# Gated delta rule on one core: four-wide inverse products, outputs taken chunk by chunk, two projection banks

## Chip, cores and metric

One core of one Trainium2 chip runs the whole program. The metric is device time in microseconds, the median of several runs. The kernel is written in a low-level language: every engine has its own list of instructions, and semaphores are written out by hand.

## What is computed

The reference is one transformer layer with post-layernorm on x of 2 x 2048 x 256, in float32. The part that the change touches is the attention, a gated delta rule over 16 heads of width 64:

```python
q, k, v = x @ Wq.T, x @ Wk.T, x @ Wv.T
q, k, v = causal_dwconv4(q), causal_dwconv4(k), causal_dwconv4(v)
g, beta = log_sigmoid(x @ Wg.T), sigmoid(x @ Wb.T)
k = k / norm(k);  q = q * 64 ** -0.5
def step(S, inp):                       # one token, S is 64 x 64 a head
    Sk = einsum('bhkv,bhk->bhv', S, k_t)
    delta = outer(v_t, k_t) - outer(Sk, k_t)
    S = exp(g_t) * S + b_t * delta
    return S, einsum('bhkv,bhk->bhv', S, q_t)
x = layernorm(x + o @ Wo.T)
x = layernorm(x + ffn(x))               # 64 experts, top 6, capacity 128, and a shared expert
```

## The kernel before, in words

The program runs five phases one after the other: gates, the delta rule, a mix phase (output projection, layernorm, routing), the experts, and the combination. The change is in the delta phase alone.

**Macros and slots.** The delta rule is computed in chunks of 64 tokens. A macro m is one pair of heads, both batches, and a span of 256 tokens: 4 chunks x 2 heads x 2 batches = 16 blocks of 64 x 64. There are 64 macros. The program is a software pipeline of 71 slots t, written out by hand for each engine (the loops `for t in range(SLOTS)`). In slot t, macro t is projected and convolved, macro t-1 is turned to tokens on partitions, gated, and its key products are taken and masked, macros t-3 and t-4 (two at a time, a group) have their 16 x 16 diagonal blocks inverted by substitution on VectorE, macro t-5 has the 64 x 64 inverse built from these, and the group (t-7)//2 does two chunks of the recurrence, here called the first and the second chain step. Slots 0 to 6 have no chain steps, slots 64 to 70 have no projections. An odd slot starts a substitution (rows 0 to 5, behind the conv of the keys), an even slot ends it (rows 6 to 14, of which 6 to 8 come ahead of the first state update).

**Partitions.** A half is 64 partitions. A matmul with 64 rows and 64 columns uses one of four tiles of the array; (rows half h, outputs half h) is called straight here, (h, other half) crossing. `QUADS` runs batch 0 straight and batch 1 crossing, so four matmuls use the four tiles. `by_unit` (L432) runs only straight ones, in pairs.

**The inverse of macro t-5.** `inverse_r` (first product, L441) multiplies the off-diagonal part with the block inverses, 48 columns; ScalarE copies the result to `rt`. `inverse_rx`, `inverse_ry1` and `inverse_ry2` (second, third and fourth product, 48, 32 and 16 columns) each follow a correction on VectorE, `horner` (L635), which subtracts the product from the block inverses. Each is 16 matmuls of `by_unit`. The block inverses come back from memory (`load_inverse`, L309), normal and transposed.

**A chain step.** `chain_state` (L461): 8 state products (key side) into `p_c`, then 8 query products into `p_d`. VectorE's `residual` takes the difference to the values. `chain_solve` (L486) multiplies it with the inverse, ScalarE's `solved` copies the solution `u`, `chain_update` (L500) makes the state increment (8) and the output products (8, added to the query products in `p_d`), and VectorE's `update` adds the increment to the decayed state that GpSimd has prepared. `p_d` gathers four chunks and ScalarE's `output` (L781) copies it once a group.

**Projections.** `project` (L360) writes keys, values and queries into the one bank `p_j`, and `exponents` (L409) writes there too. Each must wait until ScalarE has taken what was in it: `history` (L706) copies it and `last_tap` (L718) applies the last tap of the convolution.

**Scaling.** ScalarE's `scale_keys` (L768) scales the keys in eight copies of 64 columns, `scale_values` (L775) the values; GpSimd's `roots` makes the factors for the values.

The order of TensorE in a full slot is: first `chain_state`, keys' projection, first solve, turns of keys and half of the values, first update, exponents, the other half of the values, first inverse product, second `chain_state`, values' projection, second solve, second inverse product, second update, queries' projection, third inverse product, key products, fourth inverse product.

## Time and profile before

| | |
|---|---|
| median of 3 runs | 1839.55 us (1839.3 to 1841.66) |
| profiled execution | 1834.91 us, its span 1833.0 us |
| mean granted TensorE clock | 0.957 of full |
| TensorE busy | 1616.1 us, 88% |
| weight loads | 1234.2 us, 67% |
| VectorE busy | 1194.4 us, 65% |
| ScalarE busy | 909.6 us, 50% |
| GpSimd busy | 865.8 us, 47% |

The span runs from the first to the last instruction. Busy times of matmuls are modelled from their records, and consecutive matmuls overlap, so pieces of a timeline are compared by their starts. The delta phase goes from about 64 to 1222 us of the span. Every float32 matmul shows as two records. A line of a timeline merges like instructions that follow each other; "idle before" is the engine's idle time ahead of that line, with what ended it.

### The profile page before, as it was taken

How to read it: one execution, taken by the hardware profiler on the slowest of the kernel's cores; microseconds unless marked ns; L12 is line 12 of the kernel's file. 1: busy time of each engine (PE TensorE's matmuls, PEld its weight loads, DVE VectorE, ACT ScalarE, POOL GpSimd, SP SyncE). 2: the span in 40 equal slices, each digit the busy share in tenths (PEclk: the TensorE clock that was granted, in tenths of full speed). 3: DMA queues.
4: the chain of work that ended last, by engine and by line, in shares of the span. 5: the costliest groups of instructions: out<-in, count | busy, mean ns of one | idle time of the engine just before them, and what ended most of it. 6: DMA issues, size and time to landing. Idle time of an engine off the chain costs nothing. (4 is left out here: it accounts for less than half of the span.)

```text
span 1833.0 us, 74029 instructions
## 1 busy us (share of the span) xinstructions
PE 1616.1 (88%) x31244; PEld 1234.2 (67%) x31244; DVE 1194.4 (65%) x3029; ACT 909.6 (50%) x2314; POOL 865.8 (47%) x1133
## 2 busy tenths in 40 slices
PE   7479999999999999999999999759999994899950
PEld 6136666666676666667667666658888884878840
DVE  1378888888888888888888888514555553222215
ACT  1266766676676666666666666311222221333313
POOL 0034344344344344344344344214777776677853
PEclk9799999999999999999999999879999998899985
DMA  6235455556555555555555555434555551799557
GB/s 272 81 80 119 113 115 121 126 113 124 126 114 121 126 114 122 126 113 123 126 113 122 115 115 118 80 106 149 176 153 176 153 153 35 203 262 223 93 93 244
DMA packets 530218, 245.45 MB, mean 134 GB/s; under 512 B 423504, under 2 KB 497872, under 8 KB 528992
## 3 DMA queue, kind: packets, MB, share of 16 engines
q1 hardware_dynamic: 377824, 200.75, 42.1%
q10 hardware_dynamic: 133632, 20.98, 6.1%
q0 software_dynamic: 18432, 18.99, 5.9%
q8 instruction: 247, 4.05, 1.0%
q14 instruction: 83, 0.68, 0.1%
HBM read 169.29 MB, written 71.37 MB: 131 GB/s over the span
## 5 line engine op out<-in xcount | busy, mean ns | idle before, releaser
L375 PE MATMUL delta_p_j<-delta_xt,delta_w 128*128 128x512 f32 x768 | 386.2, 626 | 31.4 <-DMA delta_xt<-in_xt 17.5
L575 DVE SCALAR_TENSOR_TENSOR delta_kq<-delta_hist,cw,delta_kq 128x512 f32<-128x512 f32 x384 | 295.6, 770 | 30.7 <-ACT delta_kq L723 23.7
L716 ACT ACTIVATE delta_hist<-delta_p_j 128x512 f32<-128x512 f32 x192 | 114.8, 598 | 251.9 <-PE delta_p_j L375 248.0
L889 POOL TENSOR_TENSOR delta_sd<-state,eg_end 128x256 f32<-128x256 f32 x128 | 104.4, 815 | 283.2 <-DVE state L655 283.2
L375 PEld LDWEIGHTS delta_p_j<-delta_xt,delta_w 128*128 128x128 f32 x768 | 131.5, 191 | 146.6 <-issue 111.9
L1248 POOL DMA_INDIRECT slot_tokens<-mix_tokens,mix_slot x192 | 190.2, 990 | 62.4 <-issue 61.8
L436 PEld LDWEIGHTS delta_p_i<-delta_kkq,rt 64*64 64x64 f32 x4096 | 130.3, 135 | 73.1 <-DVE delta_kkq L639 67.9
L864 POOL TENSOR_SCALAR delta_n<-delta_n 128x8 f32<-128x8 f32 x64 | 15.5, 242 | 296.7 <-DVE delta_n L606 296.7
L436 PE MATMUL delta_p_i<-delta_kkq,rt 64*64 64x32 f32 (+1 forms) x4096 | 143.3, 214 | 13.9 <-DVE delta_kkq L639 13.5
L1371 DVE SCALAR_TENSOR_TENSOR expert_gate<-expert_gate,expert_p_h 88x256 f32<-88x256 f32 x64 | 26.7, 417 | 174.7 <-ACT expert_gate L1391 174.7
L589 DVE SCALAR_TENSOR_TENSOR delta_yv<-delta_hist,cw,delta_yv 128x512 f32<-128x512 f32 x128 | 132.5, 1035 | 8.1 <-ACT delta_yv L723 5.9
L1342 PE MATMUL expert_p_h<-expert_xbt,w 128*88 128x128 f32 x1024 | 127.3, 278 | 9.9 <-ACT expert_xbt L1385 9.0
L779 ACT ACTIVATE delta_kpv<-delta_kpv,delta_root 128x64 f32<-128x64 f32 x512 | 135.4, 346 | 0.0
L1342 PEld LDWEIGHTS expert_p_h<-expert_xbt,w 128*88 128x88 f32 x1024 | 115.6, 158 | 29.2 <-ACT expert_xbt L1385 27.5
L883 POOL TENSOR_TENSOR delta_root<-delta_n,half_power 128x8 f32<-128x8 f32 x64 | 133.9, 2093 | 0.0
L495 PEld LDWEIGHTS delta_p_c<-delta_r,delta_kkq 64*64 64x64 f32 x2048 | 71.0, 136 | 92.4 <-issue 86.4
L1036 PE MATMUL mix_p_y<-mix_wo,mix_ot 128*128 128x256 f32 x512 | 117.9, 384 | 14.8 <-DMA mix_wo<-in_wo 14.8
L773 ACT ACTIVATE delta_kpv<-delta_kpv,delta_fk 128x64 f32<-128x64 f32 x512 | 128.8, 343 | 0.5 <-POOL delta_fk L871 0.5
L647 DVE TENSOR_TENSOR delta_r<-delta_kpv,delta_p_c 128x256 f32<-128x256 f32 x128 | 53.8, 420 | 98.1 <-PE delta_p_c L470 97.1
L1310 POOL DMA_INDIRECT acc<-expert_yb,expert_tokens x64 | 100.6, 1572 | 32.2 <-ACT expert_yb L1397 17.7
L1036 PEld LDWEIGHTS mix_p_y<-mix_wo,mix_ot 128*128 128x128 f32 x512 | 96.2, 193 | 27.0 <-issue 14.9
L632 DVE TENSOR_TENSOR delta_xi<-delta_xi,delta_outer 128x15 f32<-128x15 f32 (+7 forms) x480 | 99.0, 206 | 16.4
(145 smaller groups left out, 3641.4 us busy)
## 6 DMA issues: line engine op xcount, KB each, us to landing
delta_xd<-x_scratch SPq DMA_DIRECT2D x256, 128.0 KB, 4.3
delta_w<-in_wqkv SPq DMA_DIRECT2D x64, 416.0 KB
w<-in_w SPq DMA_DIRECT2D x64, 352.0 KB
delta_eg<-eg_rows SPq DMA_DIRECT2D x128, 130.0 KB
n_scratch<-delta_kkq ACTq DMA_DIRECT2D x128, 128.0 KB
mix_ot<-ot SPq DMA_DIRECT2D x16, 1024.0 KB, 5.7
w<-in_w SPq DMA_DIRECT2D x64, 176.0 KB
ot<-delta_o SPq DMA_DIRECT2D x32, 256.0 KB
```

The source lines that it names most:

```text
L375: mm = pe.matmul(p_j[:, :], w[e][:, (ch * 3 + n) * 128:(ch * 3 + n) * 128 + 128], xt[m // 8 % 2][:, ch * 512:ch * 512 + 512], start=ch == ...
L436: mm = pe.matmul(view(p_i, g * C + first, (1, count), parts=half(sh)), view(lhs, g * C, (1, C), parts=half(sh)), view(rhs, at + g * C + fi ...
L575: ve.scalar_tensor_tensor(out, view(hist[e], i * 2 * 518 + tap, (259, 2), (1, 256)), cw[:, column:column + 1], out, ALU.mult, ALU.add).the ...
L589: ve.scalar_tensor_tensor(out, view(hist[e], 518 + tap, (259, 2), (1, 256)), cw[:, column:column + 1], out, ALU.mult, ALU.add).then_inc(co ...
L716: ac.activation(view(hist[e], n * 518 + 3, (259, 2), (1, 256)), p_j[:, :], ACT.Copy)
L773: ac.activation(kpv[:, at:at + C], kpv[:, at:at + C], ACT.Copy, scale=fk[:, g:g + 1]).then_inc(kp_out, 1)
L779: ac.activation(kpv[:, at:at + C], kpv[:, at:at + C], ACT.Copy, scale=root[:, g:g + 1]).then_inc(vp_out, 1)
L883: po.tensor_tensor(root[:, :], n2[:, :], view(s.half_power, 0, (0, 8)), ALU.pow).then_inc(small, 1)
L889: po.tensor_tensor(view(sd, 0, (128, 2), (C, 2), (1, C)), view(state, first_pair(group) * 128, (C, 2), (128, 2), (1, C)), view(s.eg_end, g ...
L1036: mm = pe.matmul(p_y[i % 2][:, 0:D], ot[i // 2 % 2][:, p * 256 + i % 2 * 128:p * 256 + i % 2 * 128 + 128], wo[:, p * D:p * D + D], start=p ...
L1248: po.indirect_dma_start(out=s.tok.ap(), out_offset=bass.IndirectOffsetOnAxis(ap=slot[i % 2][:, k:k + 1], axis=0), in_=tokens[:, i:i + 1], ...
L1342: mm = pe.matmul(p_h[e % 2][0:HALF, piece * 128:piece * 128 + 128], s.w13[:, at * 704 + ch * SI + piece * HALF:at * 704 + ch * SI + piece ...
```

## The change

The first inverse product also writes batch 1 a second time, crossing, so that `rt` holds batch 1 for both kinds of tile (24 matmuls, `p_i` grows to two banks). The second, third and fourth product then run straight for batch 0 and crossing for batch 1, in the order of `QUADS`; the fourth takes 32 columns instead of 16. The second half of the block inverses is loaded a second time into the other half of the partitions (two more loads a macro). `p_d` is dropped: the query products and the output products go into the free columns of `p_c`, with one clearing flag for all of a step's products, the query products move into `chain_solve`, behind the wait for the residual, and the output is copied after each chunk. TensorE waits for its own query products ahead of the solve and for its own increment ahead of the output products; the state update and the next step wait for the output's copy. `p_j` has two banks: keys and values use one, queries and exponents the other. In the order, the second `chain_state` goes ahead of the first inverse product, the scaling of the keys goes from ScalarE (8 instructions) to GpSimd (1) and together with the roots a slot later, and substitution rows and value scalings are placed anew.

```diff
-        p_j, p_xy, p_i, p_c, p_d = bank("p_j"), bank("p_xy", 2), bank("p_i"), bank("p_c", 2), bank("p_d", 2)
+        p_j, p_xy, p_i, p_c = bank("p_j", 2), bank("p_xy", 2), bank("p_i", 2), bank("p_c", 2)
...
+                    sp.dma_start(view(xd[e], 1024, (C, 4), (1, C), parts=half(sh ^ 1)),
+                                 bass.AP(s.x_scratch[group % 2], (e * 16 + sh * 8 + 4) * UNIT,
+                                         [[C, C], [UNIT, 4], [1, C]])).then_inc(xd_in[e], 16)
...
-                if n == 1 and m == 0:
-                    pe.wait_ge(tap_k, 1)
-                if n == 1 and m >= 1:
+                if n == 1:
+                    pe.wait_ge(tap_k, m + 1)
+                if n == 2 and m >= 1:
                     pe.wait_ge(exped, m)
-                if n == 2:
-                    pe.wait_ge(tap_v, m + 1)
...
-                        pe.wait_ge(tap_q, m)
...
-                if m + 1 < NM:
-                    pe.wait_ge(tap_k, m + 2)
-                else:
-                    pe.wait_ge(tap_q, NM)
-                pe.matmul(p_j[:, :], view(arg_l[e], 0, (1, 128), parts=(0, 82)), view(arg_r[e], 0, (1, 512), parts=(0, 82)),
...
-            def by_unit(lhs, rhs, at, first, count, done):
-                for g in range(8):
-                    for sh in range(2):
-                        mm = pe.matmul(view(p_i, g * C + first, (1, count), parts=half(sh)),
-                                       view(lhs, g * C, (1, C), parts=half(sh)),
-                                       view(rhs, at + g * C + first, (1, count), parts=half(sh)), start=True, stop=True)
-                mm.then_inc(done, 1)
             def inverse_r(m):
+                xdt = xd[m % 2]
...
                     pe.wait_ge(tt_out, m)
                 pe.wait_ge(noff_out, m + 1)
                 pe.wait_ge(xdt_in[m % 2], 32 * (m // 2 + 1))
-                by_unit(noff, xd[m % 2], 512, 0, 48, rt_done)
+                for c in range(4):
+                    for b, other in ((0, 0), (1, 1), (1, 0)):
+                        for h in range(2):
+                            unit = (b * 4 + c) * C
+                            mm = pe.matmul(view(p_i, 512 * other + (c * C if other else unit), (1, 48), parts=half(h ^ other)),
+                                           view(noff, unit, (1, C), parts=half(h)),
+                                           view(xdt, 512 + unit, (1, 48), parts=half(h)), start=True, stop=True)
+                mm.then_inc(rt_done, 1)
...
             def inverse_rx(m):
                 pe.wait_ge(rt_out, m + 1)
-                pe.wait_ge(xd_in[m % 2], 32 * (m // 2 + 1))
-                by_unit(rt, xd[m % 2], 0, 16, 48, rx_done)
+                pe.wait_ge(xd_in[m % 2], 64 * (m // 2 + 1))
+                for c in range(4):
+                    for b, h in QUADS:
+                        mm = pe.matmul(view(p_i, 512 * b + c * C + 16, (1, 48), parts=half(h ^ b)),
+                                       view(rt, 512 * b + c * C, (1, C), parts=half(h)),
+                                       view(xd[m % 2], 1024 * b + c * C + 16, (1, 48), parts=half(h)), start=True, stop=True)
+                mm.then_inc(rx_done, 1)
...
             def inverse_ry1(m):
                 pe.wait_ge(y1_out, m + 1)
-                by_unit(rt, kkq, ring(m), 32, 32, ry1_done)
+                for c in range(4):
+                    for b, h in QUADS:
+                        unit = (b * 4 + c) * C
+                        mm = pe.matmul(view(p_i, 512 * b + c * C + 32, (1, 32), parts=half(h ^ b)),
+                                       view(rt, unit, (1, C), parts=half(h)),
+                                       view(kkq, ring(m) + unit + 32, (1, 32), parts=half(h)), start=True, stop=True)
+                mm.then_inc(ry1_done, 1)
...
             def inverse_ry2(m):
                 pe.wait_ge(y2_out, m + 1)
-                by_unit(rt, kkq, ring(m), 48, 16, ry2_done)
+                for c in range(4):
+                    for b, h in QUADS:
+                        mm = pe.matmul(view(p_i, 512 * b + c * C + 32, (1, 32), parts=half(h ^ b)),
+                                       view(rt, 512 * b + c * C, (1, C), parts=half(h)),
+                                       view(kkq, ring(m) + (b * 4 + c) * C + 32, (1, 32), parts=half(h)),
+                                       start=True, stop=True)
+                mm.then_inc(ry2_done, 1)
...
             def chain_state(group, c):
...
                     pe.wait_ge(s_out, n)
+                    pe.wait_ge(o_done, n)
...
                     pe.wait_ge(gated, group * 2 + 2)
                 for q in range(2):
                     for b, h in QUADS:
...
-                                       view(state, ((pair + q) * 2 + b) * C, (1, C), parts=half(h)), start=True, stop=True)
+                                       view(state, ((pair + q) * 2 + b) * C, (1, C), parts=half(h)),
+                                       start=q == 0, stop=False, skip_group_check=True)
                 mm.then_inc(ks, 1)
-                if c == 0 and group >= 1:
-                    pe.wait_ge(o_done, group)
-                if n >= 1:
-                    pe.wait_ge(pu, n)
+            def chain_solve(group, c):
+                n, pair = group * 4 + c, first_pair(group)
+                pe.wait_ge(r_out, n + 1)
                 for q in range(2):
                     for b, h in QUADS:
-                        mm = pe.matmul(view(p_d, b * 512 + q * 256 + c * C, (1, C), parts=half(h ^ b)),
+                        pe.matmul(view(p_c, b * 512 + 384 + q * C, (1, C), parts=half(h ^ b)),
...
-                                  start=c == 0 and q == 0, stop=False, skip_group_check=True)
-                mm.then_inc(qs, 1)
-            def chain_solve(group, c):
-                n = group * 4 + c
-                pe.wait_ge(r_out, n + 1)
+                                  start=False, stop=False, skip_group_check=True).then_inc(qs, 1)
...
                     pe.wait_ge(tt_out, group * 2 + 2)
                     pe.wait_ge(first_out, group * 2 + 2)
+                pe.wait_ge(qs, 8 * n + 8)
                 for q in range(2):
...
-                                           view(r, (b * 2 + q) * C, (1, C), parts=half(sh)), start=True, stop=True)
+                                           view(r, (b * 2 + q) * C, (1, C), parts=half(sh)),
+                                           start=False, stop=False, skip_group_check=True)
                 mm.then_inc(tr, 1)
...
             def chain_update(group, c):
...
                 pe.wait_ge(u_out, n + 1)
...
-                    pe.wait_ge(kp_out, 8 * (group * 2 + 2))
+                    pe.wait_ge(kp_out, group * 2 + 2)
                 for q in range(2):
                     for b, h in QUADS:
...
-                                       view(u, (b * 2 + q) * C, (1, C), parts=half(h ^ b)), start=True, stop=True)
+                                       view(u, (b * 2 + q) * C, (1, C), parts=half(h ^ b)),
+                                       start=False, stop=False, skip_group_check=True)
                 mm.then_inc(ds, 1)
...
                     pe.wait_ge(masked, group * 2 + 2)
-                pe.wait_ge(qs, n + 1)
+                pe.wait_ge(ds, n + 1)
                 for q in range(2):
...
-                            mm = pe.matmul(view(p_d, b * 512 + q * 256 + c * C, (1, C), parts=half(sh)),
+                            mm = pe.matmul(view(p_c, b * 512 + 384 + q * C, (1, C), parts=half(sh)),
...
-                                           start=False, stop=c == 3, skip_group_check=True)
+                                           start=False, stop=True, skip_group_check=True)
                 mm.then_inc(pu, 1)
...
+                if two_:
+                    chain_state(*two_)
...
-                if two_:
-                    chain_state(*two_)
...
-            def horner(m, product, first, done):
-                dims = (C, 8), (1, C - first)
+            def horner(m, product, first, done, flipped=False):
+                dims = (C, 4), (1, C - first)
                 ve.wait_ge(product, m + 1)
-                ve.tensor_tensor(view(kkq, ring(m) + first, *dims), view(xd[m % 2], first, *dims), view(p_i, first, *dims),
-                                 ALU.subtract).then_inc(done, 1)
+                ve.tensor_tensor(view(kkq, ring(m) + first, (256, 2), *dims),
+                                 view(xd[m % 2], first, (1024 if flipped else 256, 2), *dims),
+                                 view(p_i, first, (512, 2), *dims), ALU.subtract).then_inc(done, 1)
...
                 ve.wait_ge(ds, n + 1)
+                ve.wait_ge(o_done, n + 1)
                 ve.wait_ge(sd_out, n + 1)
...
+                if even:
+                    substitute(subst_group, range(9, 12))
...
-                if even:
-                    substitute(subst_group, range(9, 11))
...
+                if even:
+                    substitute(subst_group, range(12, 13))
...
-                    substitute(subst_group, range(11, SUB - 1))
+                    substitute(subst_group, range(13, SUB - 1))
...
-                    horner(mi, ry1_done, 32, y2_out)
+                    horner(mi, ry1_done, 32, y2_out, flipped=True)
...
-            def scale_keys(m):
-                ac.wait_ge(clipped_bp, 2 * m + 2)
-                ac.wait_ge(kv_out, m + 1)
-                for g in range(8):
-                    at = ring(m) + g * C
-                    ac.activation(kpv[:, at:at + C], kpv[:, at:at + C], ACT.Copy, scale=fk[:, g:g + 1]).then_inc(kp_out, 1)
...
-            def output(group):
-                ac.wait_ge(pu, 4 * group + 4)
-                if group >= 2:
+            def output(group, c):
+                ac.wait_ge(pu, 4 * group + c + 1)
+                if c == 0 and group >= 2:
                     ac.wait_ge(o_out[group % 2], 48 * (group // 2))
-                ac.activation(view(o[group % 2], 0, (512, 2), (1, 512)), view(p_d, 0, (512, 2), (1, 512)), ACT.Copy,
-                              scale=HD ** -0.5).then_inc(o_done, 1)
+                ac.activation(view(o[group % 2], c * C, (512, 2), (256, 2), (1, C)), view(p_c, 384, (512, 2), (C, 2), (1, C)),
+                              ACT.Copy, scale=HD ** -0.5).then_inc(o_done, 1)
...
-                if is_macro(t - 2):
-                    scale_values(t - 2, range(0, 4))
+                if one:
+                    output(*one)
...
-                    scale_values(t - 2, range(4, 8))
+                    scale_values(t - 2, range(0, 4))
...
+                if two_:
+                    output(*two_)
...
-                if two_ and two_[1] == 3:
-                    output(two_[0])
+                if is_macro(t - 2):
+                    scale_values(t - 2, range(4, 8))
...
-                if is_macro(before):
-                    scale_keys(before)
...
+            def scale_keys(m):
+                po.wait_ge(kv_out, m + 1)
+                po.wait_ge(clipped_bp, 2 * m + 2)
+                po.tensor_tensor(view(kpv, ring(m), (C, 8), (1, C)), view(kpv, ring(m), (C, 8), (1, C)),
+                                 view(fk, 0, (1, 8), (0, C)), ALU.mult).then_inc(kp_out, 1)
...
+                if is_macro(t - 2):
+                    scale_keys(t - 2)
+                    roots(t - 2)
...
-                    roots(before)
```

## Rows read from the trace of the kernel before

**Rows 1.** Busy us of each engine by stretch (x instructions), first slots and full slots.

```profile
64.00:164.00 100.00, 79.63 (x1153) 40.81 (x1153) 74.13 (x144) 62.09 (x154) 30.22 (x46) 0.92 0.38 85
164.00:1144.00 980.00, 965.61 (x24460) 680.10 (x24456) 847.95 (x1934) 672.34 (x1707) 410.33 (x599) 1.00 0.56 120
```

**Rows 2.** TensorE's longest wait, 200 to 1000 us: total, times, longest.

```profile
PE delta_p_i L436 <- DVE delta_kkq L639: 6.9, 39, 0.5
```

**Rows 3.** TensorE's timeline of an odd slot: start us, us, instruction, count.

```profile
646.47 0.27 PE L470 MATMUL delta_p_c<-state,delta_kqg 64*64 64x64 f32 x2
...
650.48 0.45 PE L507 MATMUL delta_p_c<-delta_u,delta_kpv 64*64 64x64 f32 x15
650.76 0.63 PE L517 MATMUL delta_p_d<-delta_kkq,delta_u 64*64 64x64 f32 x16
...
652.54 0.30 PE L404 MATMUL delta_p_xy<-delta_w,delta_hist 64*64 64x64 f32 x8
...
652.89 1.03 PE L436 MATMUL delta_p_i<-delta_xd,noff 64*64 64x48 f32 x30
653.71 0.27 PE L470 MATMUL delta_p_c<-state,delta_kqg 64*64 64x64 f32 x2
...
653.99 0.24 PE L480 MATMUL delta_p_d<-delta_kqg,state 64*64 64x64 f32 x2
...
654.39 1.98 PE L375 MATMUL delta_p_j<-delta_xt,delta_w 128*128 128x512 f32 x4
656.30 0.68 PE L495 MATMUL delta_p_c<-delta_r,delta_kkq 64*64 64x64 f32 x16
...
657.63 0.27 PE L507 MATMUL delta_p_c<-delta_u,delta_kpv 64*64 64x64 f32 x2
...
657.99 0.63 PE L517 MATMUL delta_p_d<-delta_kkq,delta_u 64*64 64x64 f32 x16
...
660.46 1.06 PE L436 MATMUL delta_p_i<-delta_kkq,rt 64*64 64x32 f32 x30
661.31 0.33 PE L427 MATMUL delta_p_xy<-delta_kq 64*64 64x128 f32 x2
...
662.65 1.05 PE L436 MATMUL delta_p_i<-delta_kkq,rt 64*64 64x16 f32 x30 [0.16 <-DVE delta_kkq L639]
663.50 0.27 PE L470 MATMUL delta_p_c<-state,delta_kqg 64*64 64x64 f32 x2
```

**Rows 4.** Timeline of one chain step at the stage's end, all engines.

```profile
1215.73 0.46 PE L470 MATMUL delta_p_c<-state,delta_kqg 64*64 64x64 f32 x16
...
1216.73 0.68 PE L495 MATMUL delta_p_c<-delta_r,delta_kkq 64*64 64x64 f32 x16 [0.31 <-DVE delta_r L647]
1217.46 0.38 ACT L752 ACTIVATE delta_u<-delta_p_c 128x256 f32<-128x256 f32 x1 [2.79 <-PE delta_p_c L495]
...
1217.90 0.46 PE L507 MATMUL delta_p_c<-delta_u,delta_kpv 64*64 64x64 f32 x16 [0.48 <-ACT delta_u L752]
...
1218.43 0.42 DVE L655 TENSOR_TENSOR state<-delta_sd,delta_p_c 128x256 f32<-128x256 f32 x1 [1.75 <-PE delta_p_c L507]
...
1218.90 0.46 PE L470 MATMUL delta_p_c<-state,delta_kqg 64*64 64x64 f32 x16
```

**Rows 5.** VectorE's timeline around the start of an even slot.

```profile
662.57 1.23 DVE L618 TENSOR_TENSOR delta_kkq<-delta_p_xy,ex 128x1024 f32<-128x1024 f32 x1
663.80 0.29 DVE L639 TENSOR_TENSOR delta_kkq<-delta_xd,delta_p_i 128x128 f32<-128x128 f32 x1
...
669.64 0.41 DVE L655 TENSOR_TENSOR state<-delta_sd,delta_p_c 128x256 f32<-128x256 f32 x1
```

**Rows 6.** TensorE's waits for ScalarE in the first slots, 64 to 164 us.

```profile
PE delta_p_j L375 <- ACT delta_yv L723: 8.2, 7, 1.7
PE delta_p_j L417 <- ACT delta_kq L723: 5.7, 6, 1.6
PE delta_p_j L375 <- ACT delta_kq L723: 3.7, 5, 1.4
```

30 lines of the change are left out of this document (17 added, 13 removed).

## The prediction

> **What bounds the kernel now.** I read the busy shares by stretch first. In the attention stage from 164 to 1144 us the matmul engine is busy 965.6 of 980 us at full clock, VectorE 848, ScalarE 672 and GpSimd 410 [rows 1]. The reader is to see two things: TensorE sets the pace, and VectorE with 87% is close behind it. The stage is 57 of the 64 full slots. Then the waits of TensorE: in 800 us it waited 6.9 us for the last-but-one correction of the inverse, and for little else [rows 2]. So its order of issue decides, and the timeline of one slot gives the price of each piece. A slot goes from 646.47 to 663.50, 17.03 us [rows 3]; this one is odd, as is every slot in which VectorE begins a new inversion of blocks.
>
> Three readings of that timeline carry the sum. Starts are compared, since the records of matmuls overlap.
> - Sixteen products in pairs take as long with 32 columns (660.46 to 661.31, 0.85 us) as with 16 (662.65 to 663.50, 0.85) or 48 (652.89 to 653.71, 0.82) [rows 3]. The columns don't matter, the number of groups does: 0.103 to 0.106 us a pair.
> - Twelve products in groups of four (the value turns, 652.54 to 652.89) take 0.35: 0.117 a group of four [rows 3].
> - Eight products in groups of four ahead of a 128x128 projection (653.99 to 654.39) take 0.40 where the groups account for 0.23 [rows 3]: changing between the tile forms costs 0.17.
>
> **The change part by part**, per slot.
>
> *Inverse products.* The third and fourth product go from eight pairs (0.85) to four groups of four (4 x 0.117 = 0.47): -0.38 each, -0.76. The first grows from 16 to 24 matmuls: four groups of four and four pairs, 4 x (0.117 + 0.103) = 0.88, +0.06. If groups and pairs didn't flow into each other but cost twelve pairs, it would be 12 x 0.103 = 1.24, +0.42; that is the other bound, and I take the low value because the crossing tile has only half the work of the straight one. The second product loses less. What follows it, the state increment, waits for ScalarE to copy the solution: at the end of the stage, where nothing else is queued, solve to increment takes 1216.73 to 1217.90, 1.17 us [rows 4]. In the full slot solve plus second product take 656.30 to 657.63, 1.33 [rows 3]; without the product's second half TensorE would be there after 0.41 + 0.47 = 0.88 and then waits for the copy. So -0.16, not -0.38.
>
> *Self-waits.* The change makes TensorE wait for its own matmuls twice in each chain step: for the eight query products ahead of the solve, and for the increment ahead of the output products. The trace of before has no such wait. I price it by what other engines see: eight products in groups of four last 0.46 by their record, and the engine that waits for them starts 0.07 later (1217.90 + 0.46 to VectorE's 1218.43); TensorE released by ScalarE starts 0.06 after the copy's end (1217.46 + 0.38 to 1217.90) [rows 4]. So 0.46 + 0.06 = 0.52 from the first product to the first behind the wait. For the increment that was 0.28 (650.48 to 650.76) and 0.36 (657.63 to 657.99) [rows 3]: +0.24 and +0.16. The query products move from behind the state products to ahead of the solve: +0.52 in each step, against what they leave. In the first step they leave 0.40 less the 0.17 for the change of form, which stays: -0.23. In the second step they leave all 0.40, but the first inverse product now stands directly ahead of a projection and takes over the 0.17. Together +1.04 - 0.23 - 0.40 + 0.17 = +0.58, and +0.40 for the increments. The low bound of a self-wait is the groups alone (0.23 for the query products, nothing for the increment), 0.98 us a slot less; the high bound is one more record, below.
>
> Each of the eight query products also signals by itself, where one signal did before. The trace has no such row. Its bounds are nothing (the signals land while the groups run) and 0.22 us a step, about the length of one more short matmul (653.99, 0.24 less release) [rows 3]; I take nothing. The Trainium skill says otherwise: "TensorE: Matmul & The Clock Gate", section "The cost: per-tile semaphore tail", has the signals of concurrent tiles serialize, some 26 ns each. By that page seven more signals add an estimated 0.18 us a step, 24 us over 128 steps, and it advises one signal on the last product. No row here shows it.
>
> *The wait that goes.* With a shorter slot the 0.16 idle ahead of the fourth product [rows 3] closes in odd slots, where VectorE has slack: -0.17. Sum of an odd slot: -0.76 + 0.06 - 0.16 + 0.58 + 0.40 - 0.17 = -0.05.
>
> *Even slots.* The state products of the second step are moved ahead of the first inverse product, and the state update now waits until ScalarE has taken the output. In even slots VectorE is what comes late: its masking starts 0.93 before the slot (662.57 against 663.50) and the update ends at 669.64 + 0.41, 7.48 after the masking's start [rows 3, 5]. The wider last correction adds about 0.13 (0.42 for 256 columns [rows 4] against 0.29 for 128 [rows 5]). The new slot starts 0.38 after the masking's start instead of 0.93 (fourth product 0.38 shorter, its idle 0.17 gone), so the state is there at 7.48 + 0.13 - 0.38 + 0.05 = 7.28. TensorE gets to it after 6.42 (646.47 to 652.89) - 0.23 + 0.52 + 0.24 = 6.95. It stalls 0.33: +0.28 for an even slot. Behind that wait everything else of the slot is queued, so nothing hides it. If VectorE makes it up, the stall is nothing. Mean of both kinds (-0.05 + 0.28) / 2 = +0.11, times 57: +6 us.
>
> *Costs put at nothing.* In odd slots the update's wait for the output (ScalarE's copy, 0.38) falls where VectorE would idle anyway. The key scaling moves from ScalarE (8 small copies) to GpSimd (one multiplication); GpSimd has 570 of 980 us free, so up to 8.9 us a slot hide it, and the roots ahead of it are needed only later. Smaller output copies hide in ScalarE's 308 free us [rows 1]. Projections in two banks: no row of 200 to 1000 us has TensorE waiting for a bank [rows 2], so nothing in the full slots. The two added loads of the inverse hide unless the queue is late; uncovered, they would cost their issue.
>
> *The first seven slots.* Here the one bank does bind: 8.2 + 5.7 + 3.7 us of waits for ScalarE's last taps [rows 6]. About 16 of the 17.6 go. But VectorE is busy 74 of these 100 us, and the first inversions hang on blocks that go through memory. I take half, -8 (bounds -16 and 0).
>
> *The last seven slots.* Here a step is a chain of latencies, 1215.73 to 1218.90, 3.17 us [rows 4]. The query products put 0.52 into it. The update followed the increment's start by 0.53; now come 0.52 to the output products, their 0.63 [rows 3], 0.06, the copy 0.38 and 0.07, 1.66: +1.13. So +1.65 a step, +6.6 for the four steps of the last two slots. The five slots before have two steps each and inverse products between: from -1 to +3.3 a slot, I take +1, +5. Together +11 (bounds +2 and +23).
>
> **Sum**: 6 - 8 + 11 = +9 us against the profiled execution's own 1834.9, so 1844. The median of the runs shown is 4.6 above that execution: 1848.5 on its scale.
>
> **Rivals.**
> 1. *Self-waits are nearly free.* If TensorE releases itself sooner than records suggest, say half-way to the low bound, a slot loses 0.49, 57 x 0.49 = 28, and the tail 3: 9 - 31 = -22, 1817. For it: matmul ends are modelled, not measured. Against: VectorE and ScalarE see the modelled end plus 0.05 to 0.07. Chance 0.27.
> 2. *No change.* The even stall doesn't form because VectorE's order absorbs it (57 x 0.16 = 9 us less): +0, 1839.5. Chance 0.15.
> 3. *Signals serialize*, or a self-wait is longer by a record. It decides from about 0.05 us a step; at 0.22 it is 128 x 0.22 = 28: +37, 1877. Chance 0.10.
> 4. *The first inverse product runs as twelve pairs.* 57 x 0.36 = 20: +29, 1868. Against: pairs followed by groups of four elsewhere overlap. Chance 0.08.
> My forecast has 0.40. Its place is the moved query products with the two self-waits a step, against the three products that run four wide; it turns to a loss where the self-waits together cost more than about 0.82 a slot (I have 0.98 above their low bound).
>
> **From these to numbers.** Against 1839.55, 0.2% is 3.7 us, about what a measurement can tell. Faster: rival 1 and a third of rival 2, with a little of the forecast's spread, 0.34. Same: half of rival 2 and the forecast's lower edge, 0.17. Slower: the rest, 0.49. The forecast's own range is 1840 to 1858. For 8 in 10 I go from rival 1 nearly to rival 4: 1817 to 1868.
>
> **What would show it.** In the profile after: third and fourth product 0.47 us from first start to next; 0.5 from first query product to the solve, and from increment to output products; solve to second increment 1.17; waits of TensorE for the state update in every other slot; waits for last taps gone before 164 us; last steps 4.8 us. A slot mean of 17.1 is the forecast, under 16.8 rival 1, over 17.3 rival 3 or 4. I am wrong if TensorE's self-wait costs under 0.1 us, or if VectorE's or the inverse loads' waits appear where I price nothing.

## The result, and the profile after

The changed kernel takes 1864.87 us (median of 4 runs), the kernel before 1839.42 beside it: ratio 1.0149, 95% interval 1.0115 to 1.0182. It is slower, as forecast (1848), by 25 us where 9 were forecast. The profiled execution took 1864.56 us with a span of 1862.1 (before 1834.91 and 1833.0).

First the stretches of the changed kernel: first seven slots, full slots, last slots and what follows them; busy us of each engine (x instructions), granted clock, DMA share, GB/s.

```profile
64.00:154.50 90.50, 73.73 (x1153) 38.77 (x1156) 72.02 (x142) 50.31 (x106) 36.43 (x51) 0.91 0.42 93
154.50:1151.00 996.50, 943.49 (x25431) 631.35 (x25430) 845.86 (x1936) 586.16 (x1339) 502.36 (x658) 1.00 0.58 125
1151.00:1250.00 99.00, 70.44 (x1982) 59.05 (x1975) 33.88 (x99) 22.03 (x59) 19.09 (x27) 0.68 0.28 59
```

The same of the kernel before, cut at its own slots (they answer to [rows 1], which are cut at round times).

```profile
64.00:163.30 99.30, 78.93 (x1119) 40.17 (x1119) 73.53 (x142) 61.62 (x153) 29.52 (x45) 0.92 0.38 86
163.30:1144.50 981.20, 966.80 (x24515) 681.23 (x24512) 849.06 (x1936) 673.31 (x1711) 411.53 (x601) 1.00 0.56 120
1144.50:1223.00 78.50, 60.61 (x1902) 54.60 (x1898) 32.59 (x100) 22.25 (x59) 16.73 (x26) 0.87 0.32 65
```

The reader is to see: in the full slots TensorE is busy 23 us less and yet the stretch is 15 us longer, so the time is in waits; in the last slots the clock is 0.68 where it was 0.87. By stretch, after less before: first slots -8.4 from the first projection on, full slots +15.3 (17.48 a slot against 17.21), last slots +20.4 to the last output copy, the rest of the kernel +2.2, the start -0.4; together +29.1, the difference of the spans.

Single profiled executions scatter, and this limits what their means can tell. The rest of the kernel, the same code in every run here, takes from 610 to 619 us in the thirteen profiled executions, so its +2.2 is within the scatter; and the full slots of the changed kernel, which three of the experiments below leave as they are, take 17.48 to 17.59 us in the mean. The shortest slot is 17.01 in all four, so shortest slots and starts within a slot are the firmer numbers.

TensorE's waits from 200 to 1000 us in the changed kernel, in total, times, longest [rows 2 had 6.9 us for VectorE as the longest]:

```profile
PE delta_p_c L511 <- PE delta_p_c L500: 22.3, 92, 0.3
PE delta_p_c L535 <- PE delta_p_c L524: 4.2, 23, 0.2
PE delta_p_i L472 <- DVE delta_kkq L657: 2.8, 5, 0.7
```

TensorE waits for TensorE: L500 are the query products, L511 the solve, L524 the increments, L535 the output products. These are gaps between modelled ends and starts; the price is read from start to start, in the timeline of an odd slot, which answers to [rows 3] (17.18 us where that took 17.03):

```profile
645.47 0.44 PE L488 MATMUL delta_p_c<-state,delta_kqg 64*64 64x64 f32 x16
...
647.75 0.46 PE L500 MATMUL delta_p_c<-delta_kqg,state 64*64 64x64 f32 x16
648.52 0.62 PE L511 MATMUL delta_p_c<-delta_r,delta_kkq 64*64 64x64 f32 x14 [0.31 <-PE delta_p_c L500]
...
649.92 0.45 PE L524 MATMUL delta_p_c<-delta_u,delta_kpv 64*64 64x64 f32 x15
650.55 0.68 PE L535 MATMUL delta_p_c<-delta_kkq,delta_u 64*64 64x64 f32 x16 [0.18 <-PE delta_p_c L524]
...
652.97 1.09 PE L441 MATMUL delta_p_i<-delta_xd,noff 64*64 64x48 f32 x48
653.99 1.98 PE L376 MATMUL delta_p_j<-delta_xt,delta_w 128*128 128x512 f32 x4
655.90 0.46 PE L500 MATMUL delta_p_c<-delta_kqg,state 64*64 64x64 f32 x16
656.58 0.62 PE L511 MATMUL delta_p_c<-delta_r,delta_kkq 64*64 64x64 f32 x14 [0.22 <-PE delta_p_c L500]
...
660.82 0.67 PE L462 MATMUL delta_p_i<-delta_kkq,rt 64*64 64x32 f32 x32
661.31 1.08 PE L425 MATMUL delta_p_xy<-delta_kq 64*64 64x128 f32 x32
662.21 0.62 PE L472 MATMUL delta_p_i<-delta_kkq,rt 64*64 64x32 f32 x32
662.65 0.44 PE L488 MATMUL delta_p_c<-state,delta_kqg 64*64 64x64 f32 x16
```

Third inverse product 0.49 from start to start, fourth 0.44, first 1.02 with the change of form: as forecast. Query to solve 0.77 and 0.68 where 0.52 was forecast. And one step at the end of the stage, which answers to [rows 4]:

```profile
1237.23 0.71 PE L488 MATMUL delta_p_c<-state,delta_kqg 64*64 64x64 f32 x16 [0.99 <-DVE state L675]
1238.48 0.70 PE L500 MATMUL delta_p_c<-delta_kqg,state 64*64 64x64 f32 x16 [0.54 <-DVE delta_r L666]
1239.35 1.12 PE L511 MATMUL delta_p_c<-delta_r,delta_kkq 64*64 64x64 f32 x16 [0.17 <-PE delta_p_c L500]
1240.95 0.70 PE L524 MATMUL delta_p_c<-delta_u,delta_kpv 64*64 64x64 f32 x16 [0.48 <-ACT delta_u L774]
1241.74 1.12 PE L535 MATMUL delta_p_c<-delta_kkq,delta_u 64*64 64x64 f32 x16
1242.91 0.38 ACT L800 ACTIVATE delta_o<-delta_p_c 128x256 f32<-128x256 f32 x1 [2.01 <-PE delta_p_c L535]
1243.38 0.42 DVE L675 TENSOR_TENSOR state<-delta_sd,delta_p_c 128x256 f32<-128x256 f32 x1 [4.96 <-ACT delta_o L800]
1243.86 0.70 PE L488 MATMUL delta_p_c<-state,delta_kqg 64*64 64x64 f32 x16 [1.00 <-DVE state L675]
```

6.63 us a step where it was 3.17; the chain through the output copy is there as foreseen, and every product's record is longer by half or more (0.71 for 0.46, 1.12 for 0.68).

### The profile page after: what moved, and what is told of

Same layout as the page of the kernel before. It is cut to its first block and busy times, and to the rows that moved or that the text cites. A ratio compares the mean times of both kernels' runs of the same rounds, so it can differ in the third digit from the quotient of the medians.

```text
span 1862.1 us, 75918 instructions
## 1 busy us (share of the span) xinstructions
PE 1599.3 (86%) x32268; PEld 1190.0 (64%) x32268; DVE 1196.3 (64%) x3029; ACT 807.2 (43%) x1898; POOL 966.8 (52%) x1197
## 5 line engine op out<-in xcount | busy, mean ns | idle before, releaser
L593 DVE SCALAR_TENSOR_TENSOR delta_kq<-delta_hist,cw,delta_kq 128x512 f32<-128x512 f32 x384 | 290.7, 757 | 29.9 <-ACT delta_kq L745 22.8
L910 POOL TENSOR_TENSOR delta_sd<-state,eg_end 128x256 f32<-128x256 f32 x128 | 128.5, 1004 | 276.5 <-DVE state L675 275.8
L647 DVE TENSOR_TENSOR delta_outer<-delta_xi,delta_kb 128x15 f32<-128x15 f32 (+7 forms) x480 | 109.4, 228 | 23.3 <-DMA delta_kb<-n_scratch 13.3
L607 DVE SCALAR_TENSOR_TENSOR delta_yv<-delta_hist,cw,delta_yv 128x512 f32<-128x512 f32 x128 | 117.5, 918 | 3.4 <-ACT delta_yv L745 1.0
L675 DVE TENSOR_TENSOR state<-delta_sd,delta_p_c 128x256 f32<-128x256 f32 x128 | 53.6, 419 | 102.1 <-ACT delta_o L800 53.8
L511 PE MATMUL delta_p_c<-delta_r,delta_kkq 64*64 64x64 f32 x2048 | 91.6, 231 | 30.5 <-PE delta_p_c L500 30.5
L904 POOL TENSOR_TENSOR delta_root<-delta_n,half_power 128x8 f32<-128x8 f32 x64 | 107.2, 1676 | 0.0
L500 PEld LDWEIGHTS delta_p_c<-delta_kqg,state 64*64 64x64 f32 x2048 | 43.8, 139 | 95.9 <-DVE delta_r L666 65.6
L511 PEld LDWEIGHTS delta_p_c<-delta_r,delta_kkq 64*64 64x64 f32 x2048 | 74.5, 141 | 47.6 <-PE delta_p_c L500 34.2
```

Source lines behind the costliest of these rows:

```text
L511: mm = pe.matmul(view(p_c, b * 512 + 128 + q * C, (1, C), parts=half(sh)), view(kkq, ring(group * 2 + q) + b * 256 + c * C, (1, C), parts= ...
L593: ve.scalar_tensor_tensor(out, view(hist[e], i * 2 * 518 + tap, (259, 2), (1, 256)), cw[:, column:column + 1], out, ALU.mult, ALU.add).the ...
L607: ve.scalar_tensor_tensor(out, view(hist[e], 518 + tap, (259, 2), (1, 256)), cw[:, column:column + 1], out, ALU.mult, ALU.add).then_inc(co ...
L647: ve.tensor_tensor(view(outer, 0, (left, i), (1, left)), view(xi, row, (SUB, i), (0, left)), view(kb, row * SUB + row + 1, (0, i), (1, lef ...
L904: po.tensor_tensor(root[:, :], n2[:, :], view(s.half_power, 0, (0, 8)), ALU.pow).then_inc(small, 1)
L910: po.tensor_tensor(view(sd, 0, (128, 2), (C, 2), (1, C)), view(state, first_pair(group) * 128, (C, 2), (128, 2), (1, C)), view(s.eg_end, g ...
```

## The experiments

Each ratio is against the kernel before, measured beside it (medians of 1837 to 1845 us), with its 95% interval; "us" from a ratio is its difference times 1839. By the intervals, a difference against the changed kernel is good to about 7 us, one between two later runs to 4 or 5.

**One signal for the query products.** The edit:

```diff
-    pe.matmul(... query ...).then_inc(qs, 1)      # eight of them
+    mm = pe.matmul(... query ...)
+mm.then_inc(qs, 1)
-pe.wait_ge(qs, 8 * n + 8)
+pe.wait_ge(qs, n + 1)
```

> The changed kernel, but the eight query products of a slot carry one signal, on the last, in place of eight. My theory, that signals are nearly free and the self-wait is what costs: the time stays within 0.2% of the changed kernel (1861 to 1869). The rival that signals serialize: the stretch from first query product to first solve product falls from 0.77 and 0.68 us to about the 0.55 us that increments to output product take with one signal, twice a slot, so 0.35 us over 70 slots, about 1840 to 1848. The Trainium skill (TensorE: Matmul & The Clock Gate, section on the per-tile semaphore tail) says signals serialize after the matmuls; it speaks for the second.

Measured: 1.0072 (1.0053 to 1.0092), 14 us less than the changed kernel's 1.0149. Its timeline, the second step of one slot and the first of the next:

```profile
671.84 0.46 PE L500 MATMUL delta_p_c<-delta_kqg,state 64*64 64x64 f32 x16
672.39 0.62 PE L512 MATMUL delta_p_c<-delta_r,delta_kkq 64*64 64x64 f32 x14
...
680.83 0.46 PE L500 MATMUL delta_p_c<-delta_kqg,state 64*64 64x64 f32 x16
681.47 0.62 PE L512 MATMUL delta_p_c<-delta_r,delta_kkq 64*64 64x64 f32 x14 [0.18 <-PE delta_p_c L500]
```

0.55 and 0.64, each 0.13 less than with eight signals (0.68 and 0.77). The signals are not free: seven cost 0.13 us, 0.019 each, and 128 steps make 17 us of it. The ratio says 14, give or take 7. In the profiled executions the shortest slot falls by the full 0.26 (17.01 to 16.75), the mean slot only by 0.11 (17.48 to 17.37), 6.6 us in 57 slots: the stretches ahead of the fourth inverse product and of the second state products are 0.09 and 0.08 longer. So my theory fell here and the rival stood, at 0.26 a slot where it had 0.35; how much of the 17 us reaches the kernel's time is known only roughly. The Trainium skill ("TensorE: Matmul & The Clock Gate", section "The cost: per-tile semaphore tail") has 26 ns for each signal; the runs give 19 by this difference. The 0.64 belongs to the steps in which two more waits stand before this one (the first of each group of four); 0.09 for them.

**Query products behind the state products again.**

```diff
 chain_state:  ... state products
+              ... query products
 mm.then_inc(ks, 1)
 chain_solve:
-              ... query products, each .then_inc(qs, 1)
-    pe.wait_ge(qs, 8 * n + 8)
```

> The changed kernel, but the query products stand directly behind the state products, where they stood before the change, and the last of them carries the signal that VectorE and the solve product wait for, so TensorE doesn't wait for itself ahead of the solve product. If the moved query products and that self-wait are the price, each step loses about 0.5 us (0.77 and 0.68 less the 0.23 that the products take), 0.9 to 1.0 a slot: about 50 us in the steady slots and 7 in the last, 1800 to 1815. If what TensorE gives up only comes back as a wait for VectorE's right side or for the exponents, 1845 to 1860.

Measured: 1.0047 (1.0029 to 1.0065), 19 us less than the changed kernel, not 50. The shortest slots fall from 17.01 to 16.63, by less than half of the 0.9 in the expectation, and the mean only from 17.48 to 17.32; to the last step the last slots take 84.7 us for 92.9. From key products to fourth inverse product it is now 1.24 us in the median slot for 0.90 in the changed kernel, as VectorE's right side is late. TensorE's waits, 165 to 1130 us:

```profile
PE delta_p_i L472 <- DVE delta_kkq L656: 13.1, 33, 1.4
PE delta_p_c L534 <- PE delta_p_c L523: 5.2, 27, 0.2
...
PE delta_p_c L523 <- ACT delta_u L773: 3.7, 5, 1.3
```

From start to start the two places give back 0.91 us a slot, but most of it returns as other waits, the one for VectorE first. Of the 19 us about 9 are in the full slots and 8 in the last. Both halves of the expectation were partly right.

**Inverse products in pairs again**, all else as changed: in the second, third and fourth product

```diff
-view(p_i, 512 * b + ..., parts=half(h ^ b)), view(rt, 512 * b + c * C, ...)
+view(p_i, 512 * b + ..., parts=half(h)),     view(rt, unit, ...)
```

The correction ahead of the fourth product then reads the block inverses unflipped, as before the change.

> The changed kernel, but the second, third and fourth inverse products run straight in pairs of quadrants as before the change, without the crossing; the outputs that leave PSUM for each chunk and the two projection banks stay. If four side by side bring what the records show (third and fourth 0.38 us each, second up to 0.16), this is 45 to 60 us slower than the changed kernel: 1905 to 1925. If these products lie beside other work, no difference: 1865.

Measured: 1.0434 (1.0412 to 1.0456), 52 us slower than the changed kernel. Its mean full slot is 18.44, 0.96 longer. So four side by side do bring what the forecast gave them; the change loses elsewhere more than these 52 us.

**The kernel before with one self-wait.**

```diff
 mm.then_inc(ds, 1)            # increment products
+pe.wait_ge(ds, n + 1)
 ... output products
```

> The kernel before the change with one wait added: TensorE waits for its own increments ahead of the output products, in each step. Prices the self-wait alone. By the forecast's terms 0.24 and 0.16 us, 0.40 a slot, 28 us over 70 slots, and up to 5 more in the last: 1865 to 1873. If it is covered, 1840.

Measured: 1.0079 (1.0048 to 1.0109; its six times go from 1851 to 1866), +14.5 us. One place in its timeline (L507 increments, L518 output products):

```profile
688.59 0.45 PE L507 MATMUL delta_p_c<-delta_u,delta_kpv 64*64 64x64 f32 x15
689.13 0.68 PE L518 MATMUL delta_p_d<-delta_kkq,delta_u 64*64 64x64 f32 x16
689.75 1.12 PE L417 MATMUL delta_p_j<-arg_r,arg_l 82*128 82x512 f32 x2
```

The output products begin 0.55 us after the first increment (688.58), 0.29 before, and what follows them 0.62 later, 0.56 before. So 0.27 + 0.05 in each step, 0.64 a slot; 0.31 of it comes back where TensorE stood for VectorE ahead of the fourth product. The usual slot is 17.36, +0.32, and the mean slot 17.54, +0.33. The forecast had 0.40 for it and the returned wait in another term. The last slots don't lengthen by it (74.1 us against 74.3 to the last step): there the state update is on the path and the output products beside it.

**Filler in the last slots**, 80 small products a step into a bank that is free by then:

```diff
 mm.then_inc(ks, 1)
+fill(group, 6)      # groups of four, only in the last six slots
 ...
 mm.then_inc(tr, 1)
+fill(group, 4)
 ...
 mm.then_inc(pu, 1)
+fill(group, 10)
```

> The changed kernel, with filler products that nothing reads added to the chain steps of the last six slots (80 a step, into a bank that is free there), so that TensorE isn't idle while VectorE and ScalarE work. Theory of the clock: the granted clock of the last slots rises from 0.68, a product's records go from 1.12 back to about 0.7 us, a step from 6.6 to about 5 us, 10 to 15 us in all: 1850 to 1856. If the clock is not what lengthens the last steps, the filler is only in the way: 1865 to 1875.

Measured: 1.0259 (1.0243 to 1.0276), 20 us slower than the changed kernel. From 1240 to 1271 us the granted clock is 1.00 and the solve's products take 0.68 again, so the clock did what the theory says; but new stalls appear. Over the last slots TensorE stands 23.7 us with nothing in the profile that releases it, where the changed kernel has none longer than 0.15. Its timeline:

```profile
1247.40 0.62 PE L483 MATMUL delta_p_xy<-const,delta_kq 64*64 64x64 f32 x26 [1.17 <-issue]
...
1251.27 0.39 PE L483 MATMUL delta_p_xy<-const,delta_kq 64*64 64x64 f32 x10 [1.06 <-issue]
...
1255.11 0.39 PE L483 MATMUL delta_p_xy<-const,delta_kq 64*64 64x64 f32 x11 [0.93 <-issue]
...
1259.01 0.39 PE L497 MATMUL delta_p_c<-state,delta_kqg 64*64 64x64 f32 x11 [1.14 <-issue]
```

A stall each 3.84 to 3.90 us, wherever in the step it falls, released by nothing in the profile. The product records between two of them add up to 127 (1251.27 to 1255.11) and 128 (to 1259.01), with as many weight loads. And the DMA queues from 1240 to 1271 us (packets, MB, share):

```profile
q8 instruction: 8, 0.13, 1.6%
```

Eight packets of 16 KB in 31 us, one in 3.9 us: 128 product records and 128 loads for each, 64 bytes apiece. By the packets' times in the trace, each of these stalls ends 1.48 to 1.58 us after a packet has landed, and the next packet sets out 1.2 to 1.5 us after the stall's end. So I read it that TensorE runs through a packet faster than the next one comes into use; it is an inference from these times, and the next run tests it. A step has 120 products, two records each, so 240 / 128 x 3.87 = 7.3 us by this limit alone; the last three steps average 7.14 (1243.55 to 1264.96). Neither side of the expectation had this.

**The same with wide filler**: three products a step, 128x128 by 256, 192 and 384 columns.

> The changed kernel with filler that nothing reads in the last six slots again, but as three wide products a step (256, 192 and 384 columns, 128 by 128 weights) in place of 80 small ones, so TensorE is as busy with a few per cent of the instructions. In the run with small filler the clock stayed at 0.97 and yet the last slots took 19 us more; stalls of about 1.1 us came every 3.9 us, one for each 16 KB packet of the instruction queue. If instructions that come too slowly made that loss and the low clock makes the long steps of the changed kernel, the steps fall from 6.63 to about 5.0 us: 1850 to 1857. If filler is in the way whatever its form, 1870 or more. If the clock doesn't matter, 1863 to 1867.

Measured: 1.0120 (1.0101 to 1.0140), 5 us less than the changed kernel, which by the ratios alone is hardly clear, and less than the 8 to 15 expected; the last slots are 5.0 us shorter in the profile (87.9 us to the last step for 92.9). A window and two rows of its timeline:

```profile
1228.00:1247.00 19.00, 17.14 (x326) 11.25 (x326) 2.64 (x7) 2.96 (x8) 1.86 (x3) 1.00 0.04 9
```

```profile
1237.49 0.46 PE L493 MATMUL delta_p_c<-state,delta_kqg 64*64 64x64 f32 x16 [0.15 <-DVE state L685]
...
1242.58 0.46 PE L493 MATMUL delta_p_c<-state,delta_kqg 64*64 64x64 f32 x16 [0.15 <-DVE state L685]
```

The granted clock is 1.00 where the changed kernel's is 0.50, no stall for instructions is left, and a step takes 5.09 us: 1.54 less than 6.63, and 0.3 above the 4.8 that the forecast had for full clock. The filler is not in the way there: 0.07 us after VectorE's residual the query products start, 0.05 after the update the state products. Of the 0.3, 0.16 is the stretch from query to solve, 0.68 with eight signals. So of the 3.46 us that a bare step lost, 1.5 is the clock and 1.9 the chain. Over all seven slots the gain is smaller, since steps with an inverse product in them gain nothing (7.94 us against 7.8 to 8.1).

**The last six slots with their sums in the free bank.**

```diff
+LATE = 29
...
-                pe.wait_ge(qs, 8 * n + 8)
+                if group < LATE:
+                    pe.wait_ge(qs, 8 * n + 8)
...
-                ve.wait_ge(o_done, n + 1)
+                if group < LATE:
+                    ve.wait_ge(o_done, n + 1)
```

From group 29 on, the query and output products go into `p_xy` as they went into `p_d` before, with one signal a step and one copy a group; the waits of TensorE for its own products that the change brought are gone, and the state update doesn't wait for the copy.

> The changed kernel, but in the last six slots, where no projection is left, the query and output products sum in the free projection bank as they did before the change, without TensorE's waits for itself and without the state update's wait for the copy of outputs. The last slots take 20.4 us more than before; if these waits are the cause, 15 to 20 us come back: 1845 to 1850. If something else lengthens them (the crossed inverse products, the clock alone), under 5 us.

Measured: 1.0032 (1.0017 to 1.0046), 21.5 us less than the changed kernel. To the last step the last slots take 72.9 us (before 74.3, changed 92.9), the steps 3.2 again, and the clock is 0.87 as before without any filler. The waits of the shared bank, with the signals and copies that belong to them, are the cause, and the low clock came with them; which of them weighs how much this run doesn't tell.

**One projection bank**, all else as changed:

```diff
-                if n == 1:
-                    pe.wait_ge(tap_k, m + 1)
-                if n == 2 and m >= 1:
+                if n == 1 and m == 0:
+                    pe.wait_ge(tap_k, 1)
+                if n == 1 and m >= 1:
                     pe.wait_ge(exped, m)
+                if n == 2:
+                    pe.wait_ge(tap_v, m + 1)
...
-                    mm = pe.matmul(view(p_j, 512 if n == 2 else 0, (1, 512)), ...
+                    mm = pe.matmul(p_j[:, 0:512], ...
```

> The changed kernel with the projections in one bank, as before. The second bank takes 8.5 us from the first seven slots by the two traces: this is 8 us slower, 1873, with nothing in the steady slots. If the bank matters there as well, 1880 or more.

Measured: 1.0162 (1.0142 to 1.0183), 2 us slower, not told from the changed kernel or from the expected 8. In the profile the full slots begin at 162.5 us, not at 154.5, with these waits before them, as [rows 6]; after that they are as long (17.51 and 17.48). The second bank helps the first slots, and by these means nothing else. By how much is less sure than 8: from the first projection the first slots take 96.4 to 99.1 us in the three profiled executions with one bank and 90.7 to 93.4 in the ten with two, 5.7 between the means.

```profile
PE delta_p_j L378 <- ACT delta_yv L750: 9.5, 7, 1.7
PE delta_p_j L420 <- ACT delta_kq L750: 5.1, 6, 1.6
PE delta_p_j L378 <- ACT delta_kq L750: 4.6, 5, 1.4
```

**Early query products and the free bank together.**

> Query products directly behind the state products in each step (no self-wait ahead of the solve product) together with the last six slots' sums in the free bank. If the two act at separate places their gains add: 50 and 18 us, about 1797. If they overlap in the last slots, some 5 us less: 1802. Should the first bring nothing, 1847.

Measured: 1825.13 us, 0.9932 (0.9918 to 0.9945): 12.5 us faster than the kernel before and 40 faster than the changed one, the sum of its two parts (19 and 21.5). That the sum comes out is partly luck: 8 us of the first part were in the last slots, which the free bank brings back anyway, and the full slots average 17.16 here where the same code had 17.32. The expectation had the first part too large, as above. This is the best version found. Where its gain over the kernel before comes from the profile tells: 7.3 us from the first slots, which the second bank shortens, 3.2 from the full slots (17.16 against 17.21), 2.0 from the last ones. In the full slots, then, what the four-wide products save (0.93 a slot) is nearly eaten up, 0.58 by the one self-wait left and most of the rest by other waits. The shortest slots are 16.6, and TensorE now waits 16 us for VectorE:

```profile
PE delta_p_i L473 <- DVE delta_kkq L678: 16.0, 37, 1.4
```

**VectorE's right side for the fourth product moved up**, on top of that.

```diff
-conv_values(m)                  # two taps
-horner(mi, ry1_done, 32, y2_out, flipped=True)
+conv_values(m, (2,))
+horner(mi, ry1_done, 32, y2_out, flipped=True)
+conv_values(m, (1,))
```

> Query products behind the state products and the last slots' sums in the free bank (the run before that took 1825), and VectorE subtracts for the fourth inverse product between its two taps of the values, not behind both. There TensorE stands 0.34 us in most slots and 1.1 us in some (mean 1.40 us from key products to the fourth product, where the key products take 0.90), as the right side is late by the second tap (1.2 us). Theory that this order on VectorE is what limits: 0.3 to 0.45 us a slot, 17 to 25 us, 1800 to 1808. If VectorE is full and hands the wait on to the state update or the mask, within 5 us of 1825.

Measured: 0.9974 (0.9957 to 0.9991), 8 us slower than without the edit. Waits of TensorE and of VectorE in it, 165 to 1130 us:

```profile
PE delta_p_c L491 <- DVE state L697: 14.4, 27, 1.0
...
PE delta_p_i L473 <- DVE delta_kkq L678: 3.6, 10, 0.4
```

```profile
DVE delta_outer L668 <- DMA delta_kb<-n_scratch: 31.2, 23, 2.4
DVE delta_kkq L678 <- PE delta_p_i L463: 22.3, 37, 1.5
```

The wait ahead of the fourth product is gone (16.0 to 3.6), and comes back as one for the state update (2.8 to 14.4), while VectorE itself stands 22 us for the third product and 31 for blocks from memory (15.0 without the edit). This profiled execution took 1846 us, 10 above its run's median, so its waits are rather too large. VectorE is busy 88% of this stretch without the edit, and the wait that it was relieved of came up elsewhere. That the load is later because of the new order was not tested.

**And the value turns between increments and output products**: the second half of them, in the first step of a slot.

> The kernel with the split taps, and the second half of the value turns moved between the increment products and the output products of the first step, where they fill TensorE's wait for its own increments (0.60 us from first to first where eight products take 0.23). 0.3 us a slot, 17 us below the kernel with the split taps, if nothing else waits for the first step's outputs; as the outputs' copy and the state update come 0.5 us later, and the second step's state products with them, the rival is 0 to +10 us.

Measured: 0.999 (0.9969 to 1.0011), 3 us above the one before it, within the intervals. The rival of its expectation stands.

## Why the prediction was right, and where its sizes were off

The sign, the 8-in-10 range (1817 to 1868) and the ranking of places were right; the forecast's own range (1840 to 1858) was left by 7 us. The forecast's terms against means over the full slots of both traces, us a slot:

| term | forecast | measured |
|---|---|---|
| third and fourth product | -0.76 | -0.77 |
| second product | -0.16 | -0.16 |
| first product, without the change of form | +0.06 | +0.02 |
| moved query products and their self-wait | +0.58 | +0.84 |
| self-wait ahead of the output products | +0.40 | +0.58 |
| idle ahead of the fourth product | -0.17 | -0.32 |
| stall ahead of the second state products, mean of both kinds | +0.17 | +0.05 |
| all other pieces | 0 | +0.03 |
| sum | +0.11 | +0.27 |

- *Four side by side* was sized from the value turns [rows 3] and held to 0.01 us; the pairs put back cost 52 us.
- *The query products* are the mis-sized term: +0.26 over. Two steps of 0.13 for seven more signals are 0.26. The prediction said "I take nothing", on the ground that the trace had no row for it, and gave the other answer a chance of 0.10. What came true in the full slots is thus the mechanism of its third rival, at 0.13 us a step. 0.26 over 57 slots is 15 us, more than the 9 by which the full slots came out above their forecast (15.3 for 6), since idle time that closed pays back a part; the run with one signal is 14 us faster by its ratio, good to 7. The forecast chose an end of a range for an unknown cost without a row on that side; the middle, 0.11, would have been 0.02 off.
- *The self-wait itself* was 0.52 by the forecast's construction, from the record and what other engines see [rows 4]; with one signal it is 0.55, and 0.64 where more waits stand before it. The output products' side was 0.18 short: 0.60 in the first step for 0.52, 0.55 in the second, and 0.05 and 0.02 for what follows them. Where one more wait stands ahead of this one, in the first step of a group, it is 0.64; in the run with one self-wait in the kernel before, where that other wait stands behind, it is 0.56 in both kinds of slot.
- *Odd and even slots* came out the other way round. The forecast had -0.05 for an odd slot and +0.28 for an even one; measured are +0.46 (17.31 to 17.77) and +0.07 (17.12 to 17.19). The even stall of 0.33 formed only in part, 0.08 in an even slot, and no wait of TensorE for the state update longer than 0.15 us stands in the full slots, though the prediction named such waits as its sign; probably TensorE's own longer steps gave VectorE slack. The idle time ahead of the fourth product fell by 0.43 in even slots and 0.21 in odd ones, probably by the same. The odd slots pay more because they hold the first step of each group, where both self-waits are 0.09 longer, and because less of their idle time closed. That the mean of both kinds came out near is in part luck.
- *The sign "a slot mean of 17.1"* was set too low by its own sum: it starts from the 17.03 of one slot, while the mean slot of the kernel before is 17.21, so +0.11 makes 17.3. GpSimd's free time a slot is 570 us over 57 slots, 10.0 and not 8.9; nothing hangs on it.
- *First seven slots*: -8 forecast, -8.4 measured, and the waits of [rows 6] gone but for 1.4 us. The half that was taken was a guess between two bounds, and over all profiled executions the second bank is worth 5.7.
- *Last seven slots*: +11 forecast, +20.4 measured. The chain was priced at 4.8 us a step at full clock; the wide filler shows 5.09. What the forecast left out is that a TensorE that waits longer is granted less clock: 0.50 at the end, 1.2 GHz, with records of 1.12 for 0.68. The trace of before had a sign of it, 0.87 in this stretch. In a bare step the clock's part is 1.5 us of 3.46; with the waits gone, all 20 us are back.
- *The rest*, +2.2, is within what the same code scatters. The spans of the profiled executions differ by 29.1 us, the medians by 25.4.

## What to carry to other kernels

To free a bank, this change put sums of several products into shared banks, and paid with waits of TensorE for itself: 0.2 to 0.3 us of a pipelined chain each, at 0.02 us more for every further signal that the wait counts. One signal, on the last of a group, is enough. Price a wait not by the engine that waits but by what is in line behind it; and where idle time of a pace-setting engine goes, ask what the engine behind it, here VectorE at 87%, will hand back: of 0.9 us freed a slot, 0.16 was left in one profile and 0.32 in the other.

## What the runs showed of the hardware

- Instructions have a rate. With products of 64 columns in groups of four (0.117 us for four, each of two records), the 16 KB packets of TensorE's instruction queue came one in 3.9 us, and TensorE stood about 1.1 us for each. In the full slots of the changed kernel (640 to 700 us) they come 3.6 to 6.6 us apart, by the packets' times in the trace, and no such stall is there. The Trainium skill, "Runtime: NRT & Kernel Launch", section "Instruction fetch mechanics", gives the 16 KB blocks of 256 instructions, which the trace bears out; it calls the crossing "mostly hidden", which holds for the mixed work of the full slots (TensorE's unexplained waits from 165 to 1130 us sum to 6.3 us, before 5.6) and not for this stretch.
- Filler raised the granted clock of the last steps from 0.50 to 1.00 (1.2 to 2.4 GHz) in both forms; 80 small products a step lost 20 us all the same, by their instructions, and three wide ones won 5 in the last slots of the profile.
- A self-wait costs more where other waits stand ahead of it in TensorE's queue: 0.64 against 0.55 us, with two of them (query products) as with one (increments).
